# Silu in the convolution stage, one-pass softplus in the preparation and fp32 restores in strips of 32 rows, in a four-layer network on one core

## What is computed

```python
xz = x @ in_proj_w.T
xh, z = jnp.split(xz, 2, axis=-1)
xc = depthwise_conv3x3(xh, conv_w)                     # 96 channels, padding 'SAME'
xc = silu(xc + conv_b)
x_flat = xc.reshape(B, DI, L); x_t = transpose(xc, (0, 1, 3, 2)).reshape(B, DI, L)
xs = [x_flat, x_t, flip(x_flat), flip(x_t)]            # K = 4 directions
x_dbl = einsum('bkdl,kcd->bkcl', xs, x_proj_w)
dts, Bs, Cs = jnp.split(x_dbl, [R, R + N], axis=2)
dts = softplus(einsum('bkrl,kdr->bkdl', dts, dt_projs_w) + dt_projs_b)
h = h * exp(dt * A) + (dt * u) * Bt                    # scan along the positions
y = einsum('bkcn,bkn->bkc', h, Ct) + Dsk * xs
y = layernorm(sum over directions) * g + b
y = y * silu(z);  out = y @ out_proj_w.T
```

## Time and profile before

| | |
|---|---|
| median of three runs | 4313.52 us (4308.70, 4313.52, 4328.05) |
| span of the profiled execution | 4322.2 us |
| the profiled execution's own time | not given apart from its span; the slowest of the three runs, 4328.05 us, is the one run longer than that span |
| busy in the span | DVE 82%, PE 78%, ACT 63%, POOL 37% |
| first and second state-space layer | from about 580 to 1640 and from about 1643 to 2700 us of the span |
| last layer | the rest, to the end |

### The profile page before, as it was taken

The page is one execution under the profiler, slowest core; times in us unless marked ns, Lnnn a source line. Parts: engine busy times, 40 slices in busy tenths (PEclk is TensorE's granted clock), DMA queues, the critical chain, the costliest instruction groups (busy, mean ns, idle before and its releaser), DMA issues. The chain is left out here.

```text
span 4322.2 us, 110119 instructions
## 1 busy us (share of the span) xinstructions
PE 3375.4 (78%) x46784; PEld 1688.2 (39%) x46784; DVE 3524.7 (82%) x3560; ACT 2718.5 (63%) x4416; POOL 1598.8 (37%) x1151
## 2 busy tenths in 40 slices
PE   6788873157777776317777778868999999999998
PEld 4476631012222223101222222553566566666553
DVE  5555476989999967789999996759988888888882
ACT  2365628845555544865555543534899999999995
POOL 0122220079999961009999995000000000000000
PEclk9799986568888887657888877977999999999999
DMA  5334203433232210353223321451221212222211
GB/s 130 83 67 75 54 18 91 145 79 79 71 76 71 66 49 10 112 146 74 72 65 77 76 61 39 126 153 41 56 56 56 64 56 56 64 56 56 56 41 49
DMA packets 160560, 309.95 MB, mean 72 GB/s; under 512 B 69592, under 2 KB 105752, under 8 KB 156101
## 3 DMA queue, kind: packets, MB, share of 16 engines
q1 hardware_dynamic: 159124, 301.24, 27.0%
q10 hardware_dynamic: 944, 1.67, 0.2%
HBM read 194.44 MB, written 107.83 MB: 70 GB/s over the span
## 5 line engine op out<-in xcount | busy, mean ns | idle before, releaser
L2323 DVE TENSOR_REDUCE l3a_mx<-l3a_mx 128x2 f32<-128x768 f32 x1296 | 1165.1, 952 | 160.2 <-PE l3a_mx L2222 156.1
L2289 ACT ACTIVATE l3a_p<-l3a_s 128x384 f32<-128x384 f32 x2592 | 1181.5, 492 | 113.2 <-PE l3a_s L2236 105.7
L1545 POOL TENSOR_TENSOR l_scan_sc<-l_scan_s,l_scan_repc 128x768 f32<-128x768 f32 x576 | 1032.3, 1837 | 5.9 <-DVE l_scan_s L1523 5.7
L1487 ACT ACTIVATE l_scan_da<-l_scan_da,l_k_a 128x768 f32<-128x768 f32 x576 | 503.9, 875 | 627.7 <-PE l_scan_da L1407 627.6
L2236 PE MATMUL l3a_s<-l3a_q,l3a_k 125*32 125x384 f16 x10368 | 802.1, 327 | 5.8 <-DMA l3a_q<-l3a_m 3.9
L2222 PE MATMUL l3a_mx<-l3a_k,l3a_q 124*32 124x384 f16 x10368 | 672.0, 334 | 57.4 <-DMA l3a_q<-l_qx 30.4
L1407 PE MATMUL l_scan_dup<-l_scan_du,l_k_pick 96*128 96x512 bf16 (+1 forms) x1152 | 347.2, 390 | 317.6 <-DMA l_scan_dt<-l_dtp 159.1
L2248 PE MATMUL l3a_o<-l3a_p,l3a_vh 128*32 128x288 f32 x6912 | 568.7, 405 | 0.8 <-issue 0.5
L1536 POOL TENSOR_TENSOR l_scan_bup<-l_scan_dus,l_scan_repb 128x768 f32<-128x768 f32 x192 | 352.6, 1837 | 484.6 <-DMA l_scan_repc<-l_bcp 484.6
L2190 POOL TENSOR_TENSOR l3a_norm<-l3a_out,l3a_spread 128x576 f32<-128x576 f32 x24 | 34.5, 1437 | 1342.1 <-DMA l3a_spread<-l_inverses 1342.1
L1407 PE MATMUL l_scan_da<-l_scan_dt,l_k_pick 96*128 96x512 bf16 (+1 forms) x1152 | 340.6, 384 | 156.1 <-DVE l_scan_s L1523 152.6
(11 more groups left out here) (215 smaller groups left out, 4295.3 us busy)
## 6 DMA issues: line engine op xcount, KB each, us to landing
l3a_q<-l_qx SPq DMA_DIRECT2D x96, 486.0 KB
l_scan_du<-l_dup SPq DMA_DIRECT2D x144, 144.0 KB
l_scan_dt<-l_dtp SPq DMA_DIRECT2D x138, 144.0 KB
l_scan_repb<-l_bcp SPq DMA_DIRECT2D x48, 384.0 KB
l_scan_repc<-l_bcp SPq DMA_DIRECT2D x46, 384.0 KB
l_dtp<-l_prep_high_t SPq DMA_DIRECT2D x16, 432.0 KB, 3.1
l_dup<-l_prep_high_u SPq DMA_DIRECT2D x16, 432.0 KB, 3.1
l_dtp<-l_prep_middle_t SPq DMA_DIRECT2D x16, 432.0 KB, 3.1
```

The source lines that it names most:

```text
L1487: act.activation(da_ps[st % 2][:, 0:TC], da_ps[st % 2][:, 0:TC], ACT.Exp, scale=A[:, column:column + 1]).then_inc(exped, 1)
L1545: pool.tensor_tensor(SC[:, st % NSC, :], S[:, n, :], REPC[k % 2][:], ALU.mult).then_inc(weighted, 1)
L2289: act.activation(P[:, k % NP, third * SW:(third + 1) * SW], s_ps[u % NS_PS][:, 0:SW], ACT.Exp)\
L2323: dve.tensor_reduce(MX[:, qt % (NB * KT), 2 * pair:2 * pair + 2], mx_ps[n % NR][:, :, 0:RG], AX_X, ALU.max)\
```

## The change

Three parts.

1. *Convolution.* The weights are loaded with the late constants, during the group norm. A DVE tap reads one contiguous run of the padded image, 798 elements with the border columns among them, and writes such a run; DVE does five units, PE the last two strips. ACT applies `Silu` itself: on z as it leaves PSUM, and on each tapped unit twice, once in place for `U` and once in transposed order for `UT`. POOL clears only the borders and makes the diagonal matrices. The wait for the store of `u` moves to the end of the preparation.
2. *Preparation.* ACT evicts each bank with `Softplus` (dt, 96 rows) and `Copy` (B and C, 32 rows). DVE raises dt to its least value and multiplies by u. dt and dt·u are stored as fp32, once each.
3. *Scan.* dt and dt·u are loaded as fp32 into one tile `dtu` of 128 rows: two halves of 384 positions of dt on rows 0 and 32, two of dt·u on rows 64 and 96. A restore is two fp32 products, each on one strip of 32 rows, each into its own PSUM bank.

The diff, cut to its core:

```diff
-        PE_STRIPS = [(1, r) for r in range(2 * PH, H, PH)]
-        DVE_UNITS = [(0, 0), (0, 2 * PH), (0, 4 * PH), (1, 0)]
         UNIT = 2 * PH
+        DVE_UNITS = [(0, 0), (0, UNIT), (0, 2 * UNIT), (1, 0), (1, UNIT)]
+        PE_STRIPS = [(1, 2 * UNIT), (1, 2 * UNIT + PH)]
...
-                sp.dma_start(w_sb[:], t[pre + "in_wT"].rearrange("(k p) n -> p k n", p=CP)).then_inc(loaded, 16)
-                sp.dma_start(cw[:], t[pre + "conv_w"]).then_inc(loaded, 16)
-                sp.dma_start(cb[:], t[pre + "conv_b"]).then_inc(loaded, 16)
+                sp.wait_ge(gated, 3)
+                sp.dma_start(u_dram[0], U[:, 0, :]).then_inc(u_stored, 16)
                 for b in range(B):
-                    sp.wait_ge(z_gated, b + 1)
+                    sp.wait_ge(z_gated, (b + 1) * n_s // B)
                     sp.dma_start(z_dram[b], z[:, b, :]).then_inc(z_stored, 16)
-                for b in range(B):
-                    sp.wait_ge(gated, b + 1)
-                    sp.dma_start(u_dram[b], U[:, b, :]).then_inc(u_stored, 16)
+                sp.wait_ge(strip_gated, len(PE_STRIPS))
+                sp.wait_ge(gated, len(DVE_UNITS))
+                sp.dma_start(u_dram[1], U[:, 1, :]).then_inc(u_stored, 16)
                 sp.wait_ge(z_stored, 16 * B)
-                sp.wait_ge(u_stored, 16 * B)
...
+                    act.activation(z[:, b, r * W:r * W + STRIP], z_ps[n % 3][:, 0:STRIP], ACT.Silu).then_inc(z_gated, 1)
+
+                def gate_unit(j):
+                    b, r = DVE_UNITS[j]
+                    act.wait_ge(tapped, j + 1)
+                    c = tapped_rows(b, r)
+                    act.activation(image_of(U[:, b, :])[:, r:r + UNIT, :], c, ACT.Silu).then_inc(gated, 1)
+                    act.activation(turned_home(b, r, UNIT), c.rearrange("p h w -> p w h"), ACT.Silu).then_inc(turned, 1)
+
+                def gate_strip(j):
+                    b, r = PE_STRIPS[j]
+                    act.wait_ge(taps_summed, j + 1)
+                    c = c_ps[j % 2][:, 0:STRIP]
+                    act.activation(U[:, b, r * W:(r + PH) * W], c, ACT.Silu, bias=cb[:, 0:1]).then_inc(strip_gated, 1)
+                    act.activation(turned_home(b, r, PH), c.rearrange("p (h w) -> p w h", w=W), ACT.Silu,
+                                   bias=cb[:, 0:1]).then_inc(strip_turned, 1)
...
+                unit_after = {10: 0}
+                unit_after_z = {4: 1, 10: 2}
+                for n in range(n_s):
+                    if n in unit_after:
+                        gate_unit(unit_after[n])
+                    place(n)
+                for n in range(n_s):
+                    if n in unit_after_z:
+                        gate_unit(unit_after_z[n])
+                    gate_z(n)
+                gate_strip(0)
+                gate_unit(3)
+                gate_strip(1)
+                gate_unit(4)
...
-                for k in range(9):
-                    mk = dve.tensor_scalar(diag[:, k, :], eye[0:DI, 0:DI], cw[:, k:k + 1], None, ALU.mult)
-                mk.then_inc(diag_made, 1)
+                dve.wait_ge(padded, 4)
                 for b, r in DVE_UNITS:
                     dve.wait_ge(placed, placed_for(b, r + UNIT))
-                    c = image_of(conv[:, b, :])[:, r:r + UNIT, :]
+                    c = conv[:, b, r * PADW:(r + UNIT) * PADW - 2]
                     for k in range(9):
-                        src = pad[:, b, r + k // 3:r + k // 3 + UNIT, k % 3:k % 3 + W]
+                        at = (b * (H + 2) + r + k // 3) * PADW + k % 3
+                        src = flat[:, at:at + UNIT * PADW - 2]
                         if k == 0:
                             link(dve.tensor_scalar(c, src, cw[:, 0:1], cb[:, 0:1], ALU.mult, ALU.add))
                         else:
                             link(dve.scalar_tensor_tensor(c, src, cw[:, k:k + 1], c, ALU.mult, ALU.add))
                     dve.sem_inc(tapped, 1)
...
+                sp.dma_start(bias[:], t[pre + "dtb"]).then_inc(loaded, 16)
+                for n in range(UNITS):
+                    i = n % 2
+                    sp.wait_ge(taken, (n + 1) * NW * 2)
+                    sp.dma_start(bc_dram[2 * n:2 * n + 2, :, :].rearrange("a n l -> (a n) l"), T[DI:128, i, :])\
+                      .then_inc(bc_stored[i], 16)
+                    sp.wait_ge(floored, n + 1)
+                    sp.dma_start(dt_dram[n], T[0:DI, i, :]).then_inc(dt_stored[i], 16)
+                    sp.wait_ge(du_done, n + 1)
+                    sp.dma_start(du_dram[n], D[:, i, :]).then_inc(du_stored[i], 16)
+                for x in (*bc_stored, *dt_stored, *du_stored):
...
+                        bank = x_ps[m % NP][:, 0, 0:w] if w <= CH else x_ps[m % NP][:]
+                        dt, bc = T[0:DI, i, at:at + w], T[DI:128, i, at:at + w]
                         if w > CH:
-                            out = out.rearrange("p (y w) -> p y w", w=CH)
-                        act.activation(out, src, ACT.Identity, bias=bias[:, k:k + 1]).then_inc(taken, 1)
...
+                        act.activation(dt, bank[0:DI], ACT.Softplus, bias=bias[:, k:k + 1]).then_inc(taken, 1)
+                        act.activation(bc, bank[DI:128], ACT.Copy).then_inc(taken, 1)
...
+                    dve.tensor_scalar(dt, dt, DT_LEAST, None, ALU.max).then_inc(floored, 1)
+                    dve.wait_ge(floored, n + 1)
...
+                        dve.wait_ge(du_stored[i], 16 * (n // 2))
+                    dve.tensor_tensor(D[:, i, :], dt, source(n), ALU.mult).then_inc(du_done, 1)
...
+        sp.dma_start(self.cw_in[:], t[pre + "in_wT"].rearrange("(k p) n -> p k n", p=CP)).then_inc(self.conv_loaded, 16)
+        sp.dma_start(self.cw[:], t[pre + "conv_w"]).then_inc(self.conv_loaded, 16)
+        sp.dma_start(self.cb[:], t[pre + "conv_b"]).then_inc(self.conv_loaded, 16)
...
+    HALF = TC // 2
+    MID = slice(CH - HALF, CH + HALF)
...
-        DT = [s.sb(f"dt{i}", [DI, NT, TC], BF16) for i in range(2)]
-        DU = [s.sb(f"du{i}", [DI, NT, TC], BF16) for i in range(2)]
+        DTU = [s.sb(f"dtu{i}", [128, NT, HALF]) for i in range(2)]
...
+        def halves(dram, p, c, h):
+
+            at = c * TC + h * HALF
+            return dram[p, :, at:at + HALF].rearrange("(t e) l -> e t l", t=NT)
...
-                    for dst, src in ((DU, du_dram), (DT, dt_dram)):
-                        for part in range(3):
-                            sp.dma_start(dst[i][32 * part:32 * part + 32, :, :],
-                                         src[p, part, :, span(c)].rearrange("(t e) l -> e t l", t=NT))\
+                    for row, src in ((64, du_dram), (0, dt_dram)):
+                        for h in range(2):
+                            sp.dma_start(DTU[i][row + 32 * h:row + 32 * h + 32, :, :], halves(src, p, c, h))\
...
-                def restore(st, src, out, done):
+                def restore(st, row, out, done):
                     k, p, d, c, n = place(st)
                     g, tl = divmod(n, NT)
-                    for at, w in BANKS:
-                        mm = pe.matmul(out[:, at:at + w], PICK[:, g, :], src[k % 2][:, tl, at:at + w],
+                    for h in range(2):
+                        rows = slice(row + 32 * h, row + 32 * h + 32)
+                        at = MID.start + h * HALF
+                        mm = pe.matmul(out[:, at:at + HALF], PICK[rows, g, :], DTU[k % 2][rows, tl, :],
                                        start=True, stop=True)
...
-                    restore(st, DU, du_ps, du_made)
+                    restore(st, 64, du_ps, du_made)
...
-                        restore(st, DT, da_ps[st % 2], dt_made)
+                        restore(st, 0, da_ps[st % 2], dt_made)
...
-                    act.activation(da_ps[st % 2][:, 0:TC], da_ps[st % 2][:, 0:TC], ACT.Exp,
+                    act.activation(da_ps[st % 2][:, MID], da_ps[st % 2][:, MID], ACT.Exp,
...
-            dt_dram = dram(pre + "dtp", [B * ND, 3, DI, L], BF16)
-            du_dram = dram(pre + "dup", [B * ND, 3, DI, L], BF16)
+            dt_dram = dram(pre + "dtp", [B * ND, DI, L], F32)
+            du_dram = dram(pre + "dup", [B * ND, DI, L], F32)
```

More of the change, by code:

```diff
@@ L932, in _, with gate_z @@
                        .then_inc(placed, 1)
[L933 to L934 removed]
+                def gate_z(n):
+                    b, r = strips[n]
                     act.wait_ge(z_ready, n + 1)
[L936 to L940 removed]
@@ L1219 @@
+                dve.wait_ge(du_done, UNITS)
 class LateConstants:
@@ L2477, in shape_constants @@
 def shape_constants():
-    bf16 = mybir.dt.np(BF16)
     k = {}
```

286 lines of the change are left out of this document (65 added, 221 removed).

## The result

The changed kernel takes 4146.6 us (median of 4 runs, 4128.98 to 4167.54) against 4317.34 for the kernel before: a ratio of 0.9607, 95% interval 0.957 to 0.9644. The prediction was 3993 with a range of 3945 to 4100. The direction was right and the size was not: 171 us gained instead of 320. The profiled execution has a span of 4139.3 us.

A forecast was written before the change was run, and what follows sets the result against it. Convolution was taken as a chain, preparation as bound by DVE, the scan by POOL. Gains of 73 and 251 less 4 make 320 us off 4322.2: 4002, or 3993 on the median's scale, range 3945 to 4100.

The forecast's parts named there:

- 5% of the scan: Scan: share of it expected in half-clock stretches, fewer than before because PE is busier.
- The half-clock triple: Scan: three steps at half clock were put at 8.5 us against 7.05.
- my 4: Scan: expected loss over both layers, +2 us a layer.
- taken off 9: Whole kernel: profiled span 8.7 us above the median of the timed runs, so 4002 became 3993 us.
- Rival B: Scan: clock goes on flickering as now, 36% at half, 43 us a layer, 4075 us in all; chance 0.13.
- instead of 69: Preparation: 69 us a layer, first store about 14 in, 49.8 of transfer, 5 of landing and barrier.
- 332 GB/s: Preparation: rate taken for the stores, 2.06 MB a unit in 6.2 us.
- Opening, small loads and folding stay: Preparation: its start stays as before, where ACT's first bank came 9.05 us in.
- Softplus costs what Identity does: Preparation: Softplus at Identity's rate, three evictions in 2.46 us, so ACT takes 4.9 us a unit.
- instead of 55: Convolution: stage of 7.6 + 44 + 2.4 + 1.0 = 55 us, five units of 8.8 us.
- contiguous taps were put at 1.02 us: Convolution: each later DVE tap 1.02 us against 1.07 before, 0.6 for the first, 8.8 us a unit.
- Rival A: Scan: row strips run one after another, PE bounds it, 4433 us in all; chance 0.08.

The follow-up runs named there:

- Experiment 4: The changed kernel with both products of a restore on the same strip of 32 rows: 5172.74 us, ratio 1.2001.
- experiment 5: The changed kernel with each restore product reading all 128 rows, weights zero outside its strip: 4614.82 us, ratio 1.0667.
- Experiment 13: The changed kernel plus a 256-column bf16 product a step that computes nothing, a short preparation opening and taps over rows of 48: 4020.34 us, ratio 0.9341.

## Why the prediction was wrong

*The step that failed* is in the paragraph on the scan: "PE is busier than now, which speaks for fewer such stretches: I put 5% of the scan". The granted clocks of 0.85 and 0.79 are 30 and 42% at half. Measured, the mean share at half is 36%, no less than before the change. I took PE's busy share for what the clock rises with. Experiment 4 has the busiest PE of all and a clock of 0.50; experiment 5 has 0.99 at the same busy share and columns, with all 128 rows instead of 32 a source. The move from products on 96 rows to products on 32 was in the diff, and I weighed it for time only. The Trainium skill, TensorE: Matmul & The Clock Gate, section "What's actually happening", says that the clock is set by how busy TensorE has been recently; taken as the busy share of the profile, experiment 4's 0.50 at 99% contradicts it.

*A term too small beside it.* The half-clock triple was 8.5 us in the sum and measured 8.92. Passes of strips side by side are 0.80 us apart at half (1193.04 to 1193.84) and 0.63 where each of the two sources has one strip (902.75 to 903.38); I had used the single pass. By the measured numbers the loss, share at half times length times what is lost of each us, is 0.30 × 755 × (1 − 7.07/8.92) = 47 us in the first scan and 0.42 × 779 × 0.207 = 68 in the second; 124 were lost; the other 9 I have not traced. The 124 lost against my 4 are 120 of the 137 us that the span is over the forecast (4139.3 − 4002); the preparation adds 15 and the convolution 6, and the other stages gave 4 back. The median is another 16 us over: I had taken off 9 for a profiled execution that ran long, and the one of the changed kernel is 7 below its median. Rival B named the mechanism, but its price was too low (4075). That its share, the 36% of the kernel before, was met on the mean is luck: it was argued from a flicker that goes on as before, and the experiments put the share anywhere between 2% and 100% with the rows of PE's products.

*The preparation.* 77.12 and 76.00 us instead of 69: 15 us. It is bound by the stores, as forecast, but the rate was read from too short a stretch: 332 GB/s in 2 us, where the eight units together ran at

```profile
662.00:716.00 54.00, 32.79 (x64) 12.79 (x63) 31.29 (x16) 36.29 (x44) 0.00 (x0) 0.81 0.92 283
```

283, which makes 2.06 MB every 7.3 us. The DMA share was 0.92 there; where it was 0.99 the stores ran at 323 (666 to 670) and 299 (710 to 716), so 332 was also the top of the range. The first store of a unit is issued every 6.9 us (662.65 to 710.97 for seven) instead of 6.2, 5 us in all. The other 3 are the opening:

```profile
643.44 0.30 SPq L876 DMA_DIRECT2D l_u<-l_u_u  x1
...
650.08 1.59 PE L1044 MATMUL l_prep_x<-l_prep_wdt,l_prep_wxdt 12*96 12x96 f32 x8 [13.26 <-DMA l_prep_bias<-in_l_dtb]
...
656.11 1.28 ACT L1081 ACT_TABLE_LOAD   x1 [3.92 <-PE l_prep_x L1055]
657.41 1.11 ACT L1081 ACTIVATE l_prep_t<-l_prep_x,l_prep_bias 96x1024 f32<-96x1024 f32 x1
```

I wrote "Opening, small loads and folding stay". The store of u no longer ends ahead of the stage, the small loads land behind it and PE starts 4.3 us in instead of 3.0, and the table load of Softplus waits with its activation for PE's first bank. Experiment 13 took both away and came to 69.9 and 72.1. (ACT's full passes a unit were eight before, the eviction and seven more, and not seven; no term of the sum used that count.) That Softplus costs what Identity does (1.11 us for 1024 columns) was right.

*The convolution.* 58.70 and 57.57 instead of 55. The unit was 9.31 us, not 8.8: contiguous taps were put at 1.02 us and take 8.62/8 = 1.08, the upper bound's rule (elements alone, 1.11) rather than my value. Five units make 2.5 us of the 3.7. The start (595.07, 7.96 us in) and the tail held.

*Rival A* (strips one after another) did not happen: four strips worked at once. Experiment 4 is the nearest run to it: 5173 us and not 4433, although dt and dt·u still overlapped, since with one strip the clock was at half throughout.

## What to carry to other kernels

When a change puts products on fewer rows of the array, price PE at the half clock until a run shows otherwise, and compare that with the time of a step of the engine that sets the pace; a busy PE is no promise of a fast one. If PE is the late one only in the half-clock stretches, a product over all rows that computes nothing can be worth more than it costs: try it before cutting work. Take a store rate from as long a stretch as the one that you forecast.
